# State-space block: the sum over states moves from PSUM matmuls to accumulating DMAs

## What is computed

```python
xz = x @ W_in;  x_in, z = split(xz)
xc = silu(conv(x_in) @ pw_kernel + conv_bias)
x_dbl = xc @ W_x                      # delta, Bm, C
delta = softplus(delta @ W_dt + b_dt)
h = exp(delta * A) * h + delta * Bm * xc      # 8 states, scanned over positions
y = sum over the 8 states of C * h
y = (y + xc * D) * silu(z)
x = x + y @ W_out
```

## Time and profile before

| | |
|---|---|
| device time, 3 runs | 2914.62 us median (2907.15 to 2915.93) |
| span of the profiled execution | 2910.6 us, 4.0 us under that median |
| span of the core | 2910.6 us, all of it the one core's |
| busy over the span | PE 2622.9 (90%), PEld 1775.5 (61%), DVE 1977.7 (68%), ACT 1613.8 (55%), POOL 439.5 (15%) us |
| the changed block | from about 47 us to 742 us of the span |

### The profile page before, as it was taken

The page is one execution under the profiler, slowest core; times in us unless marked ns, Lnnn a source line. Parts: engine busy times, 40 slices in busy tenths (PEclk is TensorE's granted clock), DMA queues, the critical chain, the costliest instruction groups (busy, mean ns, idle before and its releaser), DMA issues. The chain is left out here.

```text
span 2910.6 us, 60882 instructions
## 1 busy us (share of the span) xinstructions
PE 2622.9 (90%) x21142; PEld 1775.5 (61%) x21143; DVE 1977.7 (68%) x4470; ACT 1613.8 (55%) x3119; POOL 439.5 (15%) x450
## 2 busy tenths in 40 slices
PE   6799999996799999999887799999999899969993
PEld 3344444443466677676676467777777645558993
DVE  2699999999577777777667467777777555661223
ACT  2666666763266666666545456666666333305553
POOL 0000000000300000000022211111110032324551
PEclk9999999998899999999887889999999889969997
DMA  4000000000100000000000100000000120002225
GB/s 118 0 1 0 0 0 0 0 1 0 37 22 21 21 16 21 20 17 21 1 15 1 41 23 21 21 21 21 21 21 11 48 90 20 14 18 66 70 70 174
DMA packets 57927, 80.55 MB, mean 28 GB/s; under 512 B 8880, under 2 KB 47058, under 8 KB 57490
## 3 DMA queue, kind: packets, MB, share of 16 engines
q1 hardware_dynamic: 51778, 62.69, 7.5%
q0 software_dynamic: 6048, 16.52, 1.8%
HBM read 63.59 MB, written 15.60 MB: 27 GB/s over the span
## 5 line engine op out<-in xcount | busy, mean ns | idle before, releaser
L1309 DVE CUSTOM_DVE_ANT_0 xa_h_scores<-xa_h_score_bank,xa_h_added 112x375 f32<-112x375 f32 x1024 | 517.7, 544 | 147.7 <-PE xa_h_score_bank L1244 133.2
L1403 ACT ACTIVATE xa_h_probs<-xa_h_scores,xa_h_negmax 112x375 f32<-112x375 f32 x1024 | 561.3, 600 | 0.8 <-DVE xa_h_negmax L1316 0.6
L1256 PEld LDWEIGHTS xa_h_turn_bank<-keep_ident,xa_h_probs 112*125 112x125 f32 x3072 | 396.2, 189 | 91.7 <-DVE xa_h_probs_t L1323 23.1
L1256 PE MATMUL xa_h_turn_bank<-keep_ident,xa_h_probs 112*125 112x112 f32 x3072 | 436.0, 278 | 9.3 <-DVE xa_h_probs_t L1323 9.0
L1323 DVE COPY xa_h_probs_t<-xa_h_turn_bank 125x448 f32<-125x448 f32 x512 | 318.8, 623 | 149.1 <-PE xa_h_turn_bank L1256 135.6
L1409 ACT ACTIVATE xa_h_probs_t<-xa_h_turn_bank 125x448 f32<-125x448 f32 x256 | 138.6, 541 | 301.4 <-PE xa_h_turn_bank L1256 301.2
L663 DVE TENSOR_TENSOR_SCAN mb_state<-mb_decay,mb_drive 128x1792 f32<-128x1792 f32 x64 | 249.4, 3896 | 0.9 <-ACT mb_decay L594 0.2
L1244 PE MATMUL xa_h_score_bank<-xa_h_keys,xa_h_queries 32*112 32x375 f32 x2048 | 231.7, 522 | 10.8 <-DVE xa_h_row_max L1309 10.2
L1269 PEld LDWEIGHTS xa_h_sums_bank<-xa_h_probs_t,xa_h_values 125*32 125x32 f32 x6144 | 141.1, 110 | 154.1 <-DVE xa_h_probs_t L1323 149.0
L455 PE MATMUL mb_y_bank<-mb_read_out,keep_ident 128*128 128x448 f32 x448 | 199.2, 592 | 33.4 <-DVE mb_read_out L679 23.7
L1269 PE MATMUL xa_h_sums_bank<-xa_h_probs_t,xa_h_values 125*32 125x112 f32 x6144 | 201.5, 264 | 14.4 <-issue 6.0
(11 more groups left out here) (366 smaller groups left out, 4055.4 us busy)
## 6 DMA issues: line engine op xcount, KB each, us to landing
xa_context<-in_ctx_t SPq DMA_DIRECT2D x64, 375.0 KB, 3.1
lm_w<-in_m_w SPq DMA_DIRECT2D x16, 512.0 KB, 9.9
lm_e_wide<-lm_result_rows SPq DMA_DIRECT2D x8, 896.0 KB, 9.5
keep_x<-in_x SPq DMA_DIRECT2D x4, 896.0 KB, 16.6
lm_latent_rows<-lm_rows SPq DMA_DIRECT2D x8, 448.0 KB, 3.2
out_x<-keep_x SPq DMA_DIRECT2D x8, 448.0 KB, 6.5
xa_mask_raw<-in_key_mask SPq DMA_DIRECT2D x1, 1312.5 KB
mb_f_pw<-in_pw SPq DMA_DIRECT2D x1, 1024.0 KB
```

The source lines that it names most:

```text
L1256: last = pe.transpose(turn_bank[(par + kc) % 2][0:KP, g * S:(g + 1) * S], probs[par][:, g, kc * KP:(kc + 1) * KP], keep.ident[0:S, 0:S])
L1309: dve.tensor_tensor_reduce(scores[par][:, g, :], score_bank[g][0:S, 0:SK], added[s][:, :], 1.0, -BIG, ALU.add, ALU.max, row_max[par][:, g: ...
L1403: act.activation(probs[par][:, g, :], scores[par][:, g, :], ACT.Exp, bias=negmax[s][:, G * c + g:G * c + g + 1]).then_inc(probs_ready, 1)
```

## The change

`y_bank`, `skip_diag` and the pair add go. The sum lives in SBUF, in `y`, of two buffers that alternate by group, as `gates` now does too. ACT writes the skip term into `y` (four activations, after its gates). POOL then adds each state's `read_out` to `y` with one accumulating DMA of 896 KB. It issues a DMA only when the one before has landed. DVE writes a `read_out` buffer when the DMA two states back has landed. The gate product of group g is one in-place instruction, run after state 2 of group g + 1. `above` is merged into `delta`. Groups are unrolled by two in the loop, to alternate buffers. POOL's `split_low` for the next group stands behind the issue of state 5's DMA.

```diff
-        skip_diag = sb("skip_diag", [128, IC, 128])
-        gates = sb("gates", [128, IC, T])
+        gates = sb("gates", [128, 2, IC, T])
-        gated_y = sb("gated_y", [128, IC, T])
-        y_bank = [psum(f"y_bank{n}", [128, 512]) for n in range(IC)]
+        y = sb("y", [128, 2, IC, T])
 # all_groups
-            group(0, 0)
-            with eng.Fori(1, GROUPS - 2) as g:
-                group(g, None)
-            group(GROUPS - 2, GROUPS - 2)
-            group(GROUPS - 1, GROUPS - 1, final=True)
+            group(0, 0, 0)
+            group(1, 1, 1)
+            with eng.Fori(1, GROUPS // 2 - 1) as i:
+                for k in range(2):
+                    group(2 * i + k, k, None)
+            group(GROUPS - 2, 0, GROUPS - 2)
+            group(GROUPS - 1, 1, GROUPS - 1, final=True)
 # POOL
+            def add_state(g, k, n):
+                pool.wait_ge(read_out_ready, N * g + n + 1)
+                if n == 0:
+                    pool.wait_ge(skipped, g + 1)
+                reuse(pool, summed, 16 * (N * g + n))
+                pool.sem_inc(add_started, 1)
+                pool.dma_start(flat(y[:, k, :, :]), flat(read_out[:, n % 2, :, :]), accum_op=ALU.add).then_inc(summed, 16)
+            def group(g, k, at, final=False):
+                for n in range(6):
+                    add_state(g, k, n)
                 if not final:
                     split_low(g + 1)
-            pool.wait_ge(loaded, LOADED)
-            for c in range(IC):
-                last = pool.tensor_scalar(skip_diag[:, c, :], keep.ident[:, :], skip_w[:, c:c + 1], None, ALU.mult)
-            last.then_inc(setup, 1)
+                for n in range(6, N):
+                    add_state(g, k, n)
 # PE: skip() and add_state() are taken out; in group()
-                        gate(g, (0, 1))
-                        skip(g)
-                        gate(g, (2, 3))
+                        gate(g, range(IC))
-                    if n != FIRST:
-                        add_state(g, n)
 # ACT
-            def read_gates(g):
-                reuse(act, gated, g)
+            def read_gates(g, k):
+                reuse(act, gated, g - 1)
+            def skip(g, k):
+                for c in range(IC):
+                    last = act.activation(y[:, k, c, :], inner[:, c, :], ACT.Copy, scale=skip_w[:, c:c + 1])
+                last.then_inc(skipped, 1)
 # ACT, softplus
+                reuse(act, decay_ready, N * (g + 1))
-                    act.activation(above[:, m, :], bank[:, 0:T], ACT.Relu, bias=b_dt[:, m:m + 1])
+                    act.activation(delta[:, m, :], bank[:, 0:T], ACT.Relu, bias=b_dt[:, m:m + 1])
 # DVE
-                if n == SECOND + 1:
-                    dve.wait_ge(pair_ready, g + 1)
-                else:
-                    reuse(dve, summed, pushes_ahead(g, n - 2))
+                reuse(dve, summed, 16 * (N * g + n - 1))
-            def add_pair(g):
-                dve.wait_ge(read_out_ready, N * g + SECOND + 1)
-                dve.tensor_tensor(flat(read_out[:, SECOND % 2, :, :]), flat(read_out[:, FIRST % 2, :, :]), flat(read_out[:, SECOND % 2, :, :]),
-                                  ALU.add).then_inc(pair_ready, 1)
-            def finish(g):
-                dve.wait_ge(summed, PUSHES * (g + 1))
+            def finish(g, k):
+                dve.wait_ge(summed, 16 * N * (g + 1))
-                for c in range(IC):
-                    last = dve.tensor_tensor(gated_y[:, c, :], y_bank[c][:, 0:T], gates[:, c, :], ALU.mult)
-                last.then_inc(gated, 1)
+                dve.tensor_tensor(flat(y[:, k, :, :]), flat(y[:, k, :, :]), flat(gates[:, k, :, :]), ALU.mult).then_inc(gated, 1)
 # DVE, group()
-                    if n == SECOND:
-                        add_pair(g)
+                    if n == 2 and not first:
+                        finish(g - 1, 1 - k)
-                finish(g)
 # DVE, behind all groups
+            finish(GROUPS - 1, 1)
```

More of the change, by code:

```diff
@@ L290, in mamba_groups @@
         rows = sb("rows", [128, 2, 2, T])
-        above, soft = sb("above", [128, IC, T]), sb("soft", [128, IC, T])
-        delta, delta_inner = sb("delta", [128, IC, T]), sb("delta_inner", [128, IC, T])
+        delta, soft = sb("delta", [128, IC, T]), sb("soft", [128, IC, T])
+        delta_inner = sb("delta_inner", [128, IC, T])
         decay = sb("decay", [128, 2, IC, G, S])
@@ L440, in spread, with project_out @@
                     pe.matmul(row_bank[k][:, 0:T], own_row[:, k * N + n, :], low_parts[:, :], start=True, stop=True).then_inc(row_done[k], 1)
-            def skip(g):
-                reuse(pe, gated, g)
-                for c in range(IC):
-                    last = pe.matmul(y_bank[c][:, 0:T], skip_diag[:, c, :], inner[:, c, :], start=True, stop=False)
-                last.then_inc(skipped, 1)
-            def add_state(g, n):
-                if n == SECOND:
-                    pe.wait_ge(pair_ready, g + 1)
-                else:
-                    pe.wait_ge(read_out_ready, N * g + n + 1)
-                for c in range(IC):
-                    last = pe.matmul(y_bank[c][:, 0:T], keep.ident[:, :], read_out[:, n % 2, c, :], start=False, stop=n == N - 1)
-                last.then_inc(summed, 1)
-            def project_out(g, half):
+            def project_out(g, k, half):
                 u = OUT_B if half else OUT_A
@@ L462, in project_out @@
                 bank = front(g, u)
-                for k in range(2):
-                    b = 2 * half + k
+                for r in range(2):
+                    b = 2 * half + r
                     for c in range(IC):
-                        last = pe.matmul(bank[0:S, k * D:(k + 1) * D], gated_y[:, c, b * S:(b + 1) * S], w_out[:, c, :],
+                        last = pe.matmul(bank[0:S, r * D:(r + 1) * D], y[:, k, c, b * S:(b + 1) * S], w_out[:, c, :],
                                          start=c == 0, stop=c == IC - 1)
@@ L489, in group @@
                             low_rank(g)
-                        project_out(g, 0) if not first else pass_over(OUT_A)
+                        project_out(g, 1 - k, 0) if not first else pass_over(OUT_A)
                     if n == 6 and not final:
@@ L496, in group @@
                             spread(g + 1, 0)
-                        project_out(g, 1) if not first else pass_over(OUT_B)
+                        project_out(g, 1 - k, 1) if not first else pass_over(OUT_B)
                         if not final:
@@ L516, in _ @@
             all_groups(pe, group)
-            project_out(GROUPS, 0)
-            project_out(GROUPS, 1)
+            project_out(GROUPS, 1, 0)
+            project_out(GROUPS, 1, 1)
         @block.scalar
@@ L595, in decays, with group @@
                 last.then_inc(decay_ready, 1)
-            def group(g, at, final=False):
+            def group(g, k, at, final=False):
                 for n in range(N):
@@ L601, in group @@
                     if n == 0:
-                        read_gates(g)
+                        read_gates(g, k)
+                        skip(g, k)
                         if not final:
@@ L647, in make_delta @@
                 dve.wait_ge(log_ready, g + 1)
-                dve.tensor_tensor(flat(delta[:, :, :]), flat(above[:, :, :]), flat(soft[:, :, :]), ALU.add).then_inc(delta_ready, 1)
+                dve.tensor_tensor(flat(delta[:, :, :]), flat(delta[:, :, :]), flat(soft[:, :, :]), ALU.add).then_inc(delta_ready, 1)
                 dve.wait_ge(delta_ready, g + 1)
```

19 lines of the change are left out of this document (4 added, 15 removed).

## The result

The changed kernel takes 2900.23 us (median of 7 runs, 2891.91 to 2904.97) against 2914.62 us (median of 7 runs, 2907.15 to 2917.58). The ratio is 0.9946, with a 95% interval of 0.993 to 0.9961. The forecast was 2872 us: the direction came, a third of the size. The profiled execution has a span of 2890.5 us, 20.1 under that of before.

What follows compares the result with a forecast made beforehand. DVE was taken to bound the groups, with PE's lateness behind it. Gains of 37.8 (groups 1 to 6), 5.7 (group 0), 2.2 (last) and 1.0 (set-up), less 4.3, gave 42.4 us: 2872 us, range 2855 to 3014.

Steps and rivals of the forecast that it cites:

- (a): PE in each group: loses seven additions and the skip product, 25.4 us of 73.5 busy, leaving 48.1.
- (b): DVE in each group: the pair add goes, 2.0 us a group gained.
- (c): DVE's gate product: one instruction of 2.03 us for four of 2.21, 0.2 us a group, waiting for nothing.
- (e): Set-up: DVE's wait for POOL's diagonal goes, 1.0 us, once.
- The unknown D: Time per link of POOL's accumulating-DMA chain: 8.2 us taken, 5.2 to 11.2 possible; chain begins to bind at 8.9.
- The end: Last gate product waits for its DMA, +2.0 us less 0.2, plus 2.5 for slow projection: 4.3 us lost.
- step (d): DVE's waits in each group shrink with PE lighter: 4.1 of 5.1 us go, 1.0 stays.
- the zero for ACT's skip term: Four skip activations on ACT, 2.2 us a group, taken as costing 0 because they stand in ACT's wait for PE.
- Rival 2: Gains stay small: PE's clock falls, waits for rows and softplus stay, about 2900 us; chance 0.14.
- Rival 1: POOL's DMA chain binds, D over 9.6; at three passes +100 us, some 3014 us; chance 0.28.
- Rival 4: DVE itself slower through DMA traffic in SBUF: 0.2 us an instruction, 40 us back, about 2912 and beyond; chance 0.01.

Runs made afterwards that it cites:

- e1: Changed kernel with each accumulating DMA moving only 16 elements a partition instead of 1,792, so the sum is incomplete; 2891.97 us, ratio to before 0.9929.
- e5: Changed kernel with unused matmuls added so PE does as many as before, in the same places; 2912.53 us, ratio to before 0.9999.
- e4: Changed kernel with one of DVE's two batch statistics moved ahead of state 6's read-out, no work added; 2886.2 us, ratio to before 0.9911.
- e2: Changed kernel with both `split_low` subtractions moved from POOL to DVE; 2869.01 us, ratio to before 0.9854.
- e8: Changed kernel with both repairs: subtractions on DVE, and ACT's skip term one state later; 2858.8 us, ratio to before 0.9817, the fastest version.
- e12: e8 with unused matmuls added so PE is as busy as before; 2883.53 us, ratio to before 0.9904.
- e9: Kernel before with only its loop of groups unrolled by two; 2912.8 us, ratio to before 0.9999.
- e10c: Kernel before with 64 accumulating DMAs of 8 KB added into an unused tile, PE still summing the states; 2913.07 us, ratio to before 1.0003.
- e7: Changed kernel with each accumulating DMA cut into two halves, the second issued when the first has landed; 2932.73 us, ratio to before 1.0064.
- e3: Changed kernel with ACT's skip term moved one state later, behind the row copy DVE waits for; 2887.71 us, ratio to before 0.9897.

## Why the prediction was right and wrong

**Right.** (a) PE's additions went, and PE's relief is worth 19.1 us of the block as made, 25.2 when repaired. (b) and (c): the pair add is gone, the product takes 2.02 and waits for nothing. (e) The first `delta` is 0.65 us earlier, forecast 1.0. The unknown D, 6.8 for 8.2, was under its threshold. Of it, 2.5 us do not depend on the bytes (2.0 at 8 KB, and 0.55 to the next issue), where 2.24 were taken. The bytes cost 4.3 us (6.3 less 2.0) where 5.98 were taken: as two reads of 917,504 bytes that is 427 GB/s in place of the 307 from the earlier trace rows, as one pass 213 GB/s. No run tells these two apart. The 0.27 and the 2.40 us of the earlier trace rows were read as one scatter's; they belong to two that follow each other, which changes the sum little. The estimate by the Trainium skill's fixed part and rate ("DMA: Bandwidth & Descriptors", anatomy of one DMA), 6.2 us with two reads, agrees with the 6.3 and speaks for two reads. The end costs 6.01 us as before's 6.17 did, where 2.0 more were forecast, and the 2.5 us for a slow projection did not come (15.3 us from product to next stage, 15.5 before).

**Wrong: step (d), the waits, and the zero for ACT's skip term.** Of 39.7 us of waits in the first seven groups 28.3 were to go; 1.7 went. I had asked who was late behind PE, found each wait covered, and did not ask what DVE's own gaps had been good for. Two causes took the places:

- *POOL starved at the shared port.* DVE's softplus wait is 4.7 us in four groups. e1 excludes the bytes; e5 leaves the DMAs in, gives the waits back, and the subtraction is short; e4 needs only 0.42 us of an instruction with one input; e2 takes the subtraction away. Worth 19.7 us by e2. The four waits alone are 18.7 us and the set-up gives 1.8; against that stand the subtractions' own time on DVE and smaller shifts of the other waits. The prediction had the rows for it: 1.02 against 1.98 us. It used them for the DMA's issue (which stayed at 0.85 us beside busy DVE) and not for the subtraction itself. The Trainium skill, "SBUF — State Buffer" (who interferes with whom), says that a DVE instruction with two SBUF inputs contends with a POOL instruction that reads SBUF, and that the shared port pair is an exclusive lock. The trace agrees in kind. That whoever issues first has the pair for the whole instruction it says of DVE's two-port modes, which are not those of these instructions. In group 3 POOL waits until one drive is over; in group 4 it is kept out over three instructions, which no sentence there covers.
- *The skip term on ACT's path.* "They stand in ACT's wait for PE" was wrong: with PE early ACT runs without a gap from the skip to the row copy of state 2, and the 2.33 us push it. The activations took the 2.3 us a group given as the upper bound, and the row copy came later by as much. DVE lost less by it, as it had that wait only in part: e8 against e2 shows 8.6 us of the block, 1.1 a group, where 0 was taken.

The repaired kernel's product at 676.1 lies 8 us ahead of the forecast's (729.03 - 46.7 gained + 2.0 for the DMA = 684.3), so the gain forecast was there to be had.

**The ledger.** Groups 1 to 6 gain 21.4 us, forecast 37.8; group 0 1.8, forecast 5.7; set-up 0.65, forecast 1.0; last group and end 0.9 gained, forecast 2.1 lost. That is 24.7 for 42.4.

**From 24.7 to 14.4.** In the profiled executions the last attention gives 8.6 us back, the stages after it gain 3.6, those ahead of it 0.4: 24.7 + 0.4 - 8.6 + 3.6 = 20.1. The medians differ by 14.4, since the profiled execution of after (2892.31) is near the fastest of its seven runs; where the others lose their 8 us no trace shows. The stop of PE is in all nine kernels with the changed code, with PE relieved or not (e5, e12), with small DMAs (e1) and with no work for POOL but DMAs (e2, e8). It is in none of the four that keep the code of before. Neither unrolling alone (e9) nor the DMAs alone (e10c) bring it. Its cause stays open. The queue of instructions moves 72 to 75 packets in the nine and 63 to 66 in the four, and two packets fall into the stop of after. That would fit code that arrives late, and doesn't show it.

**The rivals.** Rival 2 named the size, about 2900, and the place, the waits for rows and softplus that stay. Its reason explains only a small part: PE's clock did fall to 0.82 to 0.86, but e8 is the fastest at the same clock. In the first two groups it counts. There PE sat idle for 3.97 and 4.96 us before the second half of its gate matmuls (L406), which then took 4.97 and 5.26 us, against 3.27 and 3.17 in before and 3.17 twice in e12. The waits at state 2 of these groups are 4.27 and 2.50 us even in e8, and 2.61 and 0.80 before. Rival 1 did not come; e7 shows that it is real, and by an estimate from it the chain would put the product where it was at a D near 9.2 and not 9.6 (749.8 at 9.52, less 64 us for each us of D, gives 729 at 9.2). Rival 4 found nothing: beside the DMAs the drive, read-out and scan take 2.0, 2.02 and 3.89 us as before.

## What to carry to other kernels

Before counting a wait of the leading engine as gain, ask which other engine works in that gap, above all one that shares a port with it; the gap may set the moment at which that engine gets in. An instruction moved to a free engine is not free if that engine's next result is waited for: follow its queue to the next consumer, and put the moved work behind it. Try repairs together, as each alone can be eaten by the other fault (4.9 us from e3 alone, 8.6 upon e2).

## What the hardware showed unexpectedly

- A POOL subtraction of 64x448 took 1.02 us with DVE idle. Where DVE ran nothing but instructions of two SBUF inputs behind the one in which it came, its time went with the moment of arrival. At 0.93 us or more after the start of the running instruction (0.93 to 0.95 into a drive, 2.86 to 3.64 into a scan) it took 1.33 to 1.98 us and ended 0.90 to 1.17 us after the start of the next instruction, whether or not DVE had waited. At 0.59 us or less (down to 0.09 before the start) it took 7.98 to 8.67 us and ended 0.90 or 0.91 us after the start of the next instruction of one input. No run has an arrival in between without an instruction of one input behind it, and why the moment decides is not shown. Before the change the late rows fixed the moment, since cast and drive both follow the same row copy.
- Accumulating DMAs from SBUF to SBUF, issued by POOL: 2.0 us for 8 KB, 4.2 for 448 KB, 6.3 for 896 KB, and 0.55 us from landing to the next issue. They did not lengthen DVE's instructions.
- PE stopped for 6.4 to 7.1 us in a loop of a stage 1,700 us behind the edited code, and the way into that stage takes 36.7 or 41.9 us by the moment at which the clock rises. Differences under some 10 us between versions of this kernel are better read from the block's own trace than from the total.
